# A 200-column memset in front of every gather of the first graph

## The reference, cut to what matters

```python
# layer 1: 200000 edges (src, dst), sorted by dst
xn  = layernorm(x)
agg = segment_sum((xn @ M)[src], dst, 6250)
x   = x + relu(xn @ W + agg)
# layer 2: attention over 131072 edges, then a gated mixture of experts
xn2 = layernorm(x)                    # plus a feed-forward of 4 experts, top 2
x   = x + ffn(xn2, edge_index, ...)
```

## Time and profile before

| what | us |
|---|---|
| median of 3 runs (lowest, highest) | 3527.27 (3522.12, 3535.72) |
| the profiled execution, its own time | 3540.27 |
| its span, first to last instruction | 3539.0 |
| first graph's gathers, first and last start | 63.9 to 2525.6 |
| second graph's gathers, first and last start | 2571.8 to 3360.1 |

### The profile page before, as it was taken

How to read it: one execution, slowest core, us unless ns; L and a number is a source line. 1 busy time by engine, 2 the same in 40 slices (tenths; PEclk the granted TensorE clock), 3 DMA queues, 4 the chain that set the end, 5 groups by cost and what they waited for, 6 DMA issues and landing times.

```text
span 3539.0 us, 36336 instructions
## 1 busy us (share of the span) xinstructions
PE 2560.6 (72%) x10290; PEld 1708.4 (48%) x10315; DVE 2344.6 (66%) x5820; ACT 920.5 (26%) x1581; POOL 2377.0 (67%) x2827
## 2 busy tenths in 40 slices
PE   2556777767677777768877887777798787777725
PEld 1334555545555545546555555555554444443314
DVE  6677676776775555565545555555358898899957
ACT  3000111111112222211111111111145565555514
POOL 3666666666656666646666666666788888888841
PEclk9776998989888989889989888989799999999968
DMA  9676566666666666646666666666622122241147
GB/s 287 227 251 205 180 201 186 204 190 196 203 184 194 205 188 204 201 145 211 202 210 196 200 202 213 197 207 207 171 62 55 45 60 57 55 131 43 41 148 230
DMA packets 476775, 600.78 MB, mean 170 GB/s; under 512 B 72486, under 2 KB 415390, under 8 KB 474526
## 3 DMA queue, kind: packets, MB, share of 16 engines
q1 hardware_dynamic: 378766, 375.94, 32.9%
q0 software_dynamic: 97216, 219.88, 22.4%
q10 hardware_dynamic: 592, 2.64, 0.2%
HBM read 313.06 MB, written 286.79 MB: 169 GB/s over the span
## 4 chain that ended last, share of the span: by engine, by line
DVE 28%; PE 22%; another core or an unknown queue 12%; issue 9%; DMA 3%; ACT 2%; POOL 1%; SPq 0%; DVEq 0%; ACTq 0%; POOLq 0%
PE wide L1535 8%; DVE picked L901 6%; DVE g L905 6%; DVE ring L855 5%; PE wide L1585 4%; PE wide L1595 4%; PE wide L1645 3%; DVE one_hot L788 2%; DMA ring<-xn_d,srci 2%; PE wide L1554 1%; DVE by_row L996 1%; DVE by_row L1003 1%; POOL ring L1737 1%; DVE comb L1178 1%
## 5 line engine op out<-in xcount | busy, mean ns | idle before, releaser
L1737 POOL DMA_INDIRECT ring<-xn_d,srci x1611 | 1562.1, 970 | 907.6 <-issue 415.4
L855 DVE SCALAR_TENSOR_TENSOR ring<-ring,same_v,wide 128x256 f32<-128x256 f32 x1610 | 771.2, 479 | 930.7 <-remote 404.3
L1535 PE MATMUL wide<-ring,one_hot 128*128 128x256 f32 x3222 | 959.1, 435 | 381.8 <-DVE ring L855 194.1
L1535 PEld LDWEIGHTS wide<-ring,one_hot 128*128 128x128 f32 x3222 | 665.4, 216 | 632.0 <-issue 201.1
L1645 PE MATMUL wide<-tab_parts,low_hot 128*128 128x400 bf16 x3144 | 580.9, 339 | 144.6 <-DVE picked L901 102.6
L1789 POOL DMA_INDIRECT g<-tab_d,srt x500 | 496.0, 992 | 82.3 <-POOL pause L1746 49.8
L1645 PEld LDWEIGHTS wide<-tab_parts,low_hot 128*128 128x128 bf16 x3144 | 298.1, 99 | 422.2 <-issue 130.7
L1595 PE MATMUL wide<-w2s,hh 128*128 128x256 f32 x1568 | 413.5, 411 | 46.5 <-DVE yo L829 35.4
L1585 PE MATMUL wide<-xt,w1s 128*128 128x512 f32 (+1 forms) x832 | 420.3, 632 | 21.5 <-ACT hh L1264 13.9
L1264 ACT ACTIVATE hh<-wide,b1c 128x512 f32<-128x512 f32 (+1 forms) x208 | 137.6, 662 | 1000.5 <-PE wide L1585 404.3
L1595 PEld LDWEIGHTS wide<-w2s,hh 128*128 128x128 f32 x1568 | 325.5, 210 | 117.2 <-DVE yo L829 40.0
(11 more groups left out here) (369 smaller groups left out, 1778.0 us busy)
## 6 DMA issues: line engine op xcount, KB each, us to landing
run_d<-ring SPq DMA_DIRECT2D x201, 1024.0 KB
ring<-xn_d,srci POOLq DMA_INDIRECT x1611
y_d<-yo SPq DMA_DIRECT2D x196, 128.0 KB
comb<-y_d SPq DMA_DIRECT2D x28, 896.0 KB
low_row<-low_d SPq DMA_DIRECT2D x13, 1024.0 KB
sum_d<-g SPq DMA_DIRECT2D x15, 768.0 KB
g<-tab_d,srt POOLq DMA_INDIRECT x500
xn_d<-ring SPq DMA_DIRECT2D x7, 896.0 KB, 7.0
```

The lines of the kernel that those rows point to most:

```text
L855: dve_at["run", j] = step(V.scalar_tensor_tensor(out=o, in0=ring[:, (j - 1) // JC % RING, (j - 1) % JC, :], scalar=same_v[:, j:j + 1], in1 ...
L1535: mm = T.matmul(bank[pair_bank[p]][:, j % 2 * D:(j % 2 + 1) * D], one_hot[:, j // 4 % 4, j % 4, :], ring[:, j // JC % RING, j % JC, :], st ...
L1737: G.indirect_dma_start(out=ring[:, s, j % JC, :], out_offset=None, in_=xn_d, in_offset=at_rows(srci[:, j:j + 1])).then_inc(sem(f"gather{s} ...
```

## The change

Every gather of the first graph gets a memset of 200 columns of the tile `pause` in front of it on POOL, after the lock. The helper moves ahead of the first graph's loop and takes a column count; the second graph's memsets stay at 280 columns. The counter of the `paused` semaphore now runs through both graphs.

```diff
 PAUSE = 280
+VISIT_PAUSE = 200
...
+        pauses = itertools.count(1)
+
+        def pause_once(columns=PAUSE):
+            n = next(pauses)
+            if n >= 2:
+                G.wait_ge(sem("paused"), n - 1)
+            G.memset(pause[:, 0:columns], 0.0).then_inc(sem("paused"), 1)
+
...
                 if j % 2 == 0 and j >= LEAD:
                     G.wait_ge(dve_step, dve_at["run", j - LEAD])
+                pause_once(VISIT_PAUSE)
                 G.indirect_dma_start(out=ring[:, s, j % JC, :], out_offset=None, in_=xn_d,
                                      in_offset=at_rows(srci[:, j:j + 1])).then_inc(sem(f"gather{s}"), 16)
-
-        pauses = itertools.count(1)
-
-        def pause_once():
-            n = next(pauses)
-            if n >= 2:
-                G.wait_ge(sem("paused"), n - 1)
-            G.memset(pause[:, :], 0.0).then_inc(sem("paused"), 1)
```

## The result

The changed kernel takes 3512.16 us (median of 14 runs, 3494.0 to 3523.4), the kernel before 3534.0 (14 runs, 3519.52 to 3544.9); the ratio is 0.9932, 95% interval 0.9915 to 0.9949. It is faster by 0.7%, where 3563 us and slower was forecast.

What follows compares the result with a forecast made beforehand. It took PE and DVE to share the load early and PE to carry it late, with time lost in waits between them and the gathers. Delays of 26, 7 and 3 us gave 3527 + 36 = 3563 us, range 3500 to 3612.

Steps and rivals of the forecast that it cites:

- One memset, one step of POOL: First graph, POOL: a 200-column memset takes 0.27 us and mostly fills idle time; the step goes from 1.25 to 1.38 us.
- upper bound of 1.69 us: POOL's step in the first graph if the idle 0.30 us is left beside the memset.
- Stops of the lock below 401 us, waits for gathers above 145: Signs in the first graph: POOL stops less for DVE's run; PE waits longer for gathers, mostly after 1630 us.
- 62 waits of 0.8 us: PE's existing waits for gathers at a chunk's first visit, each priced 0.8 us longer, between 0.4 and 1.2 us.
- The first gather after a lock: On POOL, the gather released by DVE's run starts 0.17 to 0.43 us later; 0.3 taken.
- What of it reaches the end: Delay of PE's gather waits lengthening the first graph: 7, 3 and 26 us in its three stretches, sum 36 us.
- The clock: PE's lower busy share lowers its granted clock: up to +6 us, left at nothing against gathers landing sooner.
- faster by spreading: Rival: gathers further apart land 1 us sooner at each chunk's first visit, 3501 us; chance 0.15.
- DVE held: Rival: memsets hold up DVE's one-hot matrices, 109 us on DVE, mean over 400 ns, 3617 us; chance 0.07.
- Hidden: Rival: POOL's 449 us of slack absorb the memsets, PE's gather waits no longer, 3527 us; chance 0.25.
- POOL the bound: Rival: the memset does not fill idle time, POOL's step is 1.69 us and bounds the phase, 3786 us; chance 0.03.

Runs made afterwards that it cites:

- run 1: The 200-column memset in front of the lock instead of behind it, all else as in the changed kernel: 3453.09 us, 0.9853 of the kernel before.
- run 12: Memsets of 8 columns in front of the lock, against the kernel before: 1.0022.
- run 2: Memsets of 8 columns in place of 200, behind the lock, against the kernel before: 1.0061.
- run 5: The kernel before once more, unchanged, for a trace from the same session as later runs: 3505.66 us.
- run 7: The kernel before with gathers of half a row, which the matmul reads twice, and no memset: 0.999 of the kernel before.
- run 17: Memsets of 280 columns in front of the lock, which opens at 20 visits in place of 14, against the kernel before: 0.9972.
- runs 16 and 6: 200-column memset in front of the lock, lock at 20 visits not 14, against the kernel before: one partition of 128 (16) 0.9883, all partitions (6) 0.9848.
- run 9: The kernel before with the lock opened from 14 to 20 visits, no memsets: 1.006 of the kernel before.
- run 3: Memsets of 360 columns in place of 200, behind the lock, against the kernel before: 1.0279.

## Why the prediction was wrong

*One memset, one step of POOL: right.* 0.27 and 1.38 us were forecast, 0.28 and 1.40 are in the timeline; the memset stands in the idle 0.30 us, as the second graph's rows said. The upper bound of 1.69 us was too high by its own words: with the idle 0.30 us beside the memset the sum is 0.95 + 0.27 + 0.30 = 1.52 us; 1.69 counts the 0.16 us as well, and at 1.52 POOL would not have been the bound.

*Stops of the lock below 401 us, waits for gathers above 145: right in direction, the second too small.* 62 waits of 0.8 us more would have made 195 us; 298 were measured, in 100 waits. I had priced only the waits that were there; 38 new ones came. The place was wrong too: "most of it after 1630 us" was forecast, and 146 of the 153 us came before that.

*The first gather after a lock: within its bounds.* 0.17 to 0.43 us later, 0.3 taken; 0.21 was measured. That the place behind the lock costs is borne out: run 1 against the change and run 12 against run 2 give 0.8 and 0.4%, that is 28 and 14 us.

*What of it reaches the end: the step that failed.* "32 x 0.8 = 26 us in full", and "Sum 36 us". The waits for gathers grew by 153 us in all (298 - 145), but only by 7 in the last stretch, which was to give most of the 36 (73 to 80; run 5, the other trace of the kernel before, has 43 there). PE's idle time over the first graph grew by 4, less than the 6 between the two traces of before. In the first two stretches a wait for a gather took the place of a wait for DVE's run (194 to 86 us in all), and of smaller ones. I had allowed for this there, with a half and a quarter that still reached the end; next to nothing did. The last run came 27 us earlier instead of 36 later.

*The clock: the wrong sign, and the whole difference.* I allowed "up to +6" and set it at nothing, from the granted share being higher in the stretches in which PE is busier. PE's busy share over the first graph fell a little (1820/2479 = 73.4%, then 1789/2452 = 73.0%), and the clock rose. So what differs between stretches of different work did not hold for the same work under another pace. With idle time nearly unchanged, PE's 31 us less give the 27 us of the trace; by the medians it is 22, and two traces of the kernel before differ by 15, so the size is good to about that. Why the clock rose stays open.

*The rival 'faster by spreading': close in time (3501), wrong in mechanism.* It needed landings shorter by over 0.6 us, and fewer waits for gathers; there were more. By the landings that the traces keep (not all are there), a chunk's last gather has landed 2.95 us after its start before and 2.71 after, as medians. In run 7, with half the bytes, it is 2.38, nearly the 0.6 us, and nothing is gained; and the memset gains as much with half the bytes.

*'DVE held': the hold-up is there and costs little.* 303 to 338 ns, 20 us of busy time, where 109 us had been put, and under the 400 ns that would have told of it; the first graph got no longer by it. The Trainium skill, "SBUF — State Buffer", section "Who interferes with whom", says of VectorE in a two-port mode and GpSimd that the later of the two waits for the whole instruction of the other. The traces agree in that the matrices take longer beside longer memsets (338 ns on average beside 200 columns, 441 beside 280 in run 17). They agree less in that the length of the memset should decide: one of a single partition is almost as long (0.25 us against 0.28) and holds the matrices up by 10 ns instead of 35 (runs 16 and 6 against run 9).

*'Hidden' and 'POOL the bound':* as 'hidden' had it, PE's idle time stayed (659 and 663 us), but not because the delays went unseen: PE's waits for gathers doubled, which 'hidden' had ruled out. At a step of 1.53 us (run 3) the slack no longer sufficed, 1.0279.

## What to carry to other kernels

An engine with slack that runs ahead and is then stopped by a lock can be worth slowing down, to a step still a little under that of its consumers. Here, in one kernel, 0.15 us more a step (1.40, where the gathers of that kernel come every 1.47 to 1.49 us on average) gave 1.5%, and 0.06 more took most of it back, so the size is to be swept and not reasoned out. The delay is to stand where the engine would be stopped anyway, in front of the lock; behind it the same delay gave half. When a wait of PE is priced, first look at which other wait it replaces, then at the busy time of the same matmuls before and after: here PE's work had no fixed duration.

## What the runs showed of the hardware

A memset of 128 x 200 between two indirect gathers costs 0.15 us of POOL's time and not 0.28, since it fills the idle 0.30 us behind each gather; one of 128 x 8 costs 0.01. Met waits on POOL's sequencer do not space gathers evenly: three per gather vanish in the step and start the first gather behind a lock 0.5 us later, eight come out as bursts at 1.25 us and idle gaps of 1.8. The same 832 matmuls of 128 x 512 took 596 to 632 ns on average from kernel to kernel, by the share of them that fell to the lower clock: in all 20 traces those wholly at the higher level took 565 to 569 ns, those wholly at the lower one 1016 to 1077.
